# Rotary division on GpSimd in the narrow attentions of a two-layer decoder on one core

## The reference, cut

```python
# self: 32 query heads, 8 key heads, causal, rotary by halves of a head
q = rope(x @ Wq); k = repeat(rope(x @ Wk), 4); v = repeat(x @ Wv, 4)
w = softmax(where(causal, -inf, q @ k.T) / 4);  out = (w @ v) @ Wo
# cross: 32 key heads from ctx, no mask, rotary by pairs, angles from fside
q = rope2(x @ Wq); k = rope2(ctx @ Wk); v = ctx @ Wv
w = softmax(q @ k.T / 4);  out = (w @ v) @ Wout + bout
```

## Time and profile before

| | us |
|---|---|
| median of 3 runs | 3669.28 (3666.15 to 3674.68) |
| profiled execution, its own time | 3672.33 |
| its span | 3670.5 |
| TensorE busy | 3299.7 (90%) |
| VectorE busy | 2050.8 (56%) |
| ScalarE busy | 1330.1 (36%) |
| GpSimd busy | 569.7 (16%) |

### The profile page before, as it was taken

The page is one execution under the profiler, slowest core; times in us unless marked ns, Lnnn a source line. Parts: engine busy times, 40 slices in busy tenths (PEclk is TensorE's granted clock), DMA queues, the critical chain, the costliest instruction groups (busy, mean ns, idle before and its releaser), DMA issues. The chain is left out here.

```text
span 3670.5 us, 54520 instructions
## 1 busy us (share of the span) xinstructions
PE 3299.7 (90%) x19769; PEld 2526.3 (69%) x19770; DVE 2050.8 (56%) x4964; ACT 1330.1 (36%) x2944; POOL 569.7 (16%) x621
## 2 busy tenths in 40 slices
PE   6999999999999999977958899889898857999995
PEld 6888888888888788843425565555455435787784
DVE  3555655566666666651155666666666645443445
ACT  0444434443444344431113343435444442122110
POOL 1333322222222222033141111210000000000000
PEclk7999999999999999988978999989999978999998
DMA  5111111111011011034340000000000011000001
GB/s 190 53 53 53 53 53 30 35 35 30 30 35 35 27 33 30 1 117 163 130 140 2 2 3 2 28 2 22 5 5 5 2 46 24 24 11 11 23 11 46
DMA packets 110615, 146.79 MB, mean 40 GB/s; under 512 B 23712, under 2 KB 72864, under 8 KB 109288
## 3 DMA queue, kind: packets, MB, share of 16 engines
q1 hardware_dynamic: 95904, 110.80, 9.4%
q0 software_dynamic: 14480, 32.91, 2.9%
HBM read 100.55 MB, written 42.08 MB: 39 GB/s over the span
## 5 line engine op out<-in xcount | busy, mean ns | idle before, releaser
L554 ACT ACTIVATE probs_w<-probs_w,low_w 128x256 f32<-128x256 f32 (+1 forms) x512 | 242.9, 475 | 589.7 <-DVE low_w L599 589.7
L1871 DVE TENSOR_REDUCE mx_n<-bank 128x6 f32<-128x768 f32 (+1 forms) x256 | 279.7, 1093 | 151.0 <-PE bank L1648 83.0
L1779 ACT ACTIVATE probsT_n<-bank 128x768 f32<-128x768 f32 (+1 forms) x256 | 235.8, 921 | 277.0 <-PE bank L1660 276.8
L572 DVE TENSOR_TENSOR probsT_lo_w<-bank,probsT_hi_w 128x384 fp32r<-128x384 f32 (+1 forms) x256 | 159.7, 624 | 125.7 <-ACT probsT_hi_w L537 124.9
L518 PE MATMUL bank<-wo_hi_w,oT_hi_w 128*128 128x512 f32 x512 | 211.4, 413 | 2.1 <-issue 2.1
L1642 PE MATMUL bank<-kT_n,qT_n 48*128 48x256 f32 (+1 forms) x1024 | 124.0, 322 | 94.2 <-DVE mx_n L1871 91.5
L518 PE MATMUL bank<-wo_hi_w,oT_lo_w 128*128 128x512 f32 x512 | 204.4, 399 | 0.0
L518 PE MATMUL bank<-wo_lo_w,oT_hi_w 128*128 128x512 f32 x512 | 204.4, 399 | 0.0
L582 DVE TENSOR_SCALAR probs_w<-probs_w,inv_w 128x256 f32<-128x256 f32 (+1 forms) x512 | 187.6, 408 | 20.8 <-issue 0.9
L2309 DVE SCALAR_TENSOR_TENSOR h<-bank,scale_now,silu 128x512 f32<-128x512 f32 x64 | 48.0, 750 | 202.5 <-PE bank L2202 202.5
L450 PE MATMUL bank<-xT_lo_w,wq_hi_w 128*128 128x512 f32 x512 | 161.1, 396 | 0.0
(11 more groups left out here) (362 smaller groups left out, 8141.3 us busy)
## 6 DMA issues: line engine op xcount, KB each, us to landing
expert_rows<-ctxT_hi_w SPq DMA_DIRECT2D x20, 512.0 KB, 4.3
work_m<-expert_rows SPq DMA_DIRECT2D x40, 256.0 KB, 2.6
expert_products<-work_m POOLq DMA_DIRECT2D x40, 256.0 KB, 2.7
staging_w<-in_L_attn_Wq SPq DMA_DIRECT2D x32, 256.0 KB, 3.0
expert_table<-ctxT_hi_w SPq DMA_DIRECT2D x16, 512.0 KB, 5.5
staging_w<-in_L_attn_Wo SPq DMA_DIRECT2D x32, 256.0 KB, 2.6
staging_w<-in_L_xattn_Wq SPq DMA_DIRECT2D x32, 256.0 KB, 2.6
staging_w<-in_L_xattn_Wo SPq DMA_DIRECT2D x32, 256.0 KB, 2.6
```

Of the source, the lines that this page charges most:

```text
L554: last = act.activation(pr, pr, ACT.Exp, bias=low[:, n % ROUNDS_OF_PROBS, tile:tile + 1], scale=-1.0, accum_out=den[:, n % ROUNDS_OF_PROBS ...
L572: return dve.tensor_tensor(dst, src, hi.bitcast(FP32), ALU.subtract)
L1779: act.activation(probsT[:, turn_ % SLOT_PAIRS, :, 0:cols], scoreT[:, :, 0:cols], ACT.Exp, scale=SCALE)\
L1871: dve.tensor_reduce(to.rearrange("p t h -> p h t"), seen, AX.X, ALU.max).then_inc(s["scores_read"], 1)
```

## The change

The second half of a rotation moves from VectorE to GpSimd. VectorE keeps the three products that read the bank, and tells by a new semaphore `turned` that they are done. GpSimd's new `divide` makes the sum, the rounding and the remainder and sets `split`. `rot` and `turn` get two buffers, taken in turn by the number of the rotation (k0, k1, q0, q1 of each item), and VectorE waits before a rotation until the one two before it is divided. The wait for the transposes of the keys, before parts of q are written, moves along. GpSimd now goes through the steps as the other engines do: at each step first `hide` (self items), then the divisions of that step, then context loads at step 11, then the weight loads. `var`, `rstd` and `newton` become slices of one tile.

```diff
-    rot, turn = sb("rot", [P, DIM]), sb("turn", [P, DIM])
+    rot, turn = sb("rot", [P, 2, DIM]), sb("turn", [P, 2, DIM])
+    rotation = lambda name, n: 4 * n + (2 if name[0] == "q" else 0) + int(name[1])
...
+            def divide(name, n):
+                t, q = int(name[1]), name[0] == "q"
+                heads_ = NH if q else kv_heads(n)
+                r, u = (by_head(a, name, n) for a in (rot, turn))
+                pool.wait_ge(s["turned"], rotation(name, n) + 1)
+                pool.tensor_tensor(r, r, u, ALU.add)
+                if q:
+                    pool.wait_ge(s["prep_ready"], max(uses.ready[f"kT{t}{i}", n] for i in turns(n)))
+                pool.drain()
+                twice = r.unsqueeze(2).to_broadcast([P, heads_, 2, HW])
+                if q or cross(n):
+                    d = parts[:, t, :, :].rearrange("p h (a w) -> p h a w", w=HW)
+                    hi, lo = d[:, :, 0:3:2, :] if q else d[:, :, 0:2, :], d[:, :, 1 if q else 2, :]
+                    pool.tensor_copy(hi.bitcast(FP32R), twice)
+                    pool.drain()
+                    last = pool.tensor_tensor(lo, r, d[:, :, 0, :], ALU.subtract)
+                else:
+                    d = parts[:, t, 0:2 * heads_, :].rearrange("p (h c) (a w) -> p c h a w", c=2, w=HW)
+                    for i in range(2):
+                        pool.tensor_copy(d[:, i, :, 0:2, :].bitcast(FP32R), twice)
+                    pool.drain()
+                    for i in range(2):
+                        last = pool.tensor_tensor(d[:, i, :, 2, :], r, d[:, 0, :, 0, :], ALU.subtract)
+                last.then_inc(s["split"], 1)
...
+            for n in range(-1, ITEMS):
+                for at in range(PAIRS):
+                    if 0 <= n < BATCH:
+                        hide(n, at)
+                    early, late = step(n, at)
+                    for name, item in early + late:
+                        if name in ("k0", "k1", "q0", "q1"):
+                            divide(name, item)
+                        elif name == "ctxT" and batch_of(item) + 1 < BATCH:
+                            load_context(batch_of(item) + 1)
...
+                if turn_ >= 2:
+                    dve.wait_ge(s["split"], turn_ - 1)
                 dve.tensor_tensor(r, b, wide(cos, HW), ALU.mult)
...
                 last.then_inc(s["prep_dve"], 1)
-                dve.drain()
-                dve.tensor_tensor(r, r, u, ALU.add)
-                dve.drain()
...
+                dve.drain().then_inc(s["turned"], 1)
```

More of the change, by code:

```diff
@@ L1490, in attention_narrow @@
     ident16, own16 = sb("ident16", [P, P], BF16), sb("own16", [P, P], BF16)
-    stat, var, rstd, newton = sb("stat", [P, TILES, 8]), sb("var", [P, TILES]), sb("rstd", [P, TILES]), sb("newton", [P, TILES])
+    stat, roots = sb("stat", [P, TILES, 8]), sb("roots", [P, 3, TILES])
+    var, rstd, newton = (roots[:, i, :] for i in range(3))
     score, scoreT = chip.banks[0], chip.banks[1]
@@ L1498, in attention_narrow, with by_head @@
     half = lambda h, rows: slice(64 * (h % 2), 64 * (h % 2) + rows)
+    rotation = lambda name, n: 4 * n + (2 if name[0] == "q" else 0) + int(name[1])
+    def by_head(a, name, n):
+        heads_ = NH if name[0] == "q" else kv_heads(n)
+        return a[:, rotation(name, n) % 2, 0:heads_ * HW].rearrange("p (h w) -> p h w", w=HW)
     masked = lambda bank: bank.rearrange("p (a b) -> p a b", b=SEQ)[:, :, 0:P]
@@ L1506, in attention_narrow @@
             "wq_cross_loaded", "wk_cross_loaded", "wv_cross_loaded", "wo_cross_loaded", "bias_loaded", "ctx_loaded", "consts_ready",
-            "prep_ready", "prep_act", "prep_dve", "split", "scores_ready", "scores_read", "neg_ready",
+            "prep_ready", "prep_act", "prep_dve", "turned", "split", "scores_ready", "scores_read", "neg_ready",
             "negA_there", "negB_there", "negC_there", "scoresT_ready", "exp_ready", "hidden", "values_ready", "heads_copied", "x_ready")}
@@ new lines, in _ @@
+            pool.wait_ge(s["consts_ready"], 1)
+            for name, n in before:
+                if name in ("k0", "k1"):
+                    divide(name, n)
+            for n in range(-1, ITEMS):
[8 more added lines that the diff above has]
+                            load_context(batch_of(item) + 1)
+                    if (n, at) == (BATCH - 3, PAIRS - 1):
@@ L1554, in _ @@
                         pool.wait_ge(s["prep_ready"], uses.ready["k1", BATCH - 1])
                         pool.dma_start(wk(BATCH), k_dram.rearrange("(c p) n -> p c n", p=P)).then_inc(s["wk_cross_loaded"], 16)
-                    if (n, pair) == (BATCH - 2, 7):
+                    if (n, at) == (BATCH - 2, 7):
                         pool.wait_ge(s["prep_ready"], uses.ready["q1", BATCH - 1])
                         pool.dma_start(wq[:, :, :], q_dram.rearrange("(c p) n -> p c n", p=P)).then_inc(s["wq_cross_loaded"], 16)
-                    if (n, pair) == (BATCH - 2, PAIRS - 1):
+                    if (n, at) == (BATCH - 2, PAIRS - 1):
@@ L1560, in _ @@
                         pool.wait_ge(s["prep_ready"], uses.ready["v1", BATCH - 1])
                         pool.dma_start(wv(BATCH), v_dram.rearrange("(c p) n -> p c n", p=P)).then_inc(s["wv_cross_loaded"], 16)
[L1562 to L1566, removed]
+                    if (n, at) == (BATCH, 7):
+                        pool.wait_ge(s["prep_ready"], uses.ready["out1", BATCH - 1])
+                        pool.dma_start(wo[:, :, :], o_dram.rearrange("(c p) n -> p c n", p=P)).then_inc(s["wo_cross_loaded"], 16)
@@ L1830, in rotate @@
                 wide = lambda a, w: a.unsqueeze(1).to_broadcast([P, heads_, w])
-                r = rot[:, 0:width].rearrange("p (h w) -> p h w", w=HW)
-                u = turn[:, 0:width].rearrange("p (h w) -> p h w", w=HW)
+                turn_ = rotation(name, n)
+                r, u = (by_head(a, name, n) for a in (rot, turn))
+                if turn_ >= 2:
+                    dve.wait_ge(s["split"], turn_ - 1)
                 dve.tensor_tensor(r, b, wide(cos, HW), ALU.mult)
```

## The result

The changed kernel takes 3625.8 us in the median of four runs (3616.0 to 3627.2), against 3670.7 us for the kernel before: a ratio of 0.987, 95% interval [0.985, 0.988]. So it is faster by 1.2 to 1.5%, 45 us, where 54 us were forecast. The profiled execution took 3627.2 us, its span is 3625.4 us.

What follows compares the result with a forecast made beforehand. TensorE was taken to bound the narrow attentions, waiting for maxima late on VectorE. Terms 5 + 8 + 3 + 15 + 27 - 4 = 54 us took the profiled 3672.3 us to 3618, as median 3615; range 3572 to 3655.

Steps and rivals of the forecast that it cites:

- What bounds: Narrow attentions: TensorE bounds, so a change on VectorE is worth only what TensorE waits for it.
- GpSimd's division: Sum, rounding and remainder of a 512-wide rotation on GpSimd: 4.1 us with the handover, against 2.3 us on VectorE.
- rival 2: GpSimd's four-dimensional operations on 16-element rows cost more than flat ones: 3640 us (chance 0.12) or 3680 us (0.10).
- Start: Before the first scores nothing covers the latency of GpSimd's divisions in a row: 4 us lost.
- Cross k: Key rotations of cross items: scores wait less for maxima, one slow-clock stretch goes; 3.4 us x 8 = 27 us gained.
- Cross q0: q0 rotation of cross items: earlier negations, idle split in two, half the slow clock recovered; 15 us gained.
- Self q0: q0 rotation of self items: values start 0.6 us earlier, slow clock stays; 5 us over 8 items.
- Self k: Key rotations of self items: waits for maxima go, 0.4 us returns at the negation; 8 us gained.
- First item behind q1: First self item: the 3.26 us wait behind q1 goes, with no hide in the way; 3 us gained.
- The lock: SBUF held exclusively for a whole GpSimd instruction: each VectorE negation operation can lose a whole GpSimd operation.
- Signs named ahead: Expected profile marks: shorter maxima wait, new negation and values waits, slower negations, granted clock 0.97 cross, about 0.92 self.
- Rival 1: Negations slip between GpSimd's operations and the clock recovers everywhere: 106 us gained, 3563 us; chance 0.20.

Runs made afterwards that it cites:

- twice: The full change with GpSimd's 1024-element rounding made a second time in each division: 3656.5 us, 0.995.
- cross_k: The full change with only the keys of the cross items divided on GpSimd: 3639.1 us, 0.991.
- cross_only: The full change with only the rotations of the cross items divided on GpSimd, those of the self items on VectorE: 3617.3 us, 0.986.
- self_only: The full change with only the rotations of the self items divided on GpSimd: 3671.1 us, 0.999.
- q0_later: The full change, but GpSimd divides q0 one step later, behind hide 1 and after that step's negations: 3581.8 us, 0.975.
- k_yield: `q0_later`, with GpSimd also waiting between sum and rounding of k0 until the negations of pair 5 are done: 3595.9 us, 0.980.
- hide_first: `q0_later` without the wait for the negations, so GpSimd divides q0 right after hide 1: 3614.3 us, 0.984.

## Why the prediction was right, and where not

The mechanism held in the cross items, where all of the gain lies; the term of the self items failed, and that the sum came out near is in part luck.

- **What bounds.** Right: VectorE lost 110 us of busy time and ScalarE none, and only what TensorE waited and the clock behind its waits turned into time.
- **GpSimd's division**, 4.1 us taken: 3.8 us from the sum's start to the remainder's end (2151.17 to 2155.01). Right, and rival 2 with it fell: no operation on short rows was slow. `twice` puts its turning point at an estimated 5.6 us, near the 5.5 that I named; at 5.0 us a division it took more than the half of the gain that I gave it.
- **Start**, 4 us: 5.1 us. The missing 1 us is that the projections of q0 and q1 took 8.05 us where they had taken 7.03: from 1934.1 to 1942.2 us the granted clock is 0.87, in the same work before it was 1.00.
- **Cross k**, 27 us: 34 to 36 us (`cross_k`). The mechanism was right, the term too small, and by its idle time: over items 7 to 14 TensorE idles 21 us less, where 1.3 us in each of 8 items, 10 us, were counted; its busy time fell by 15 us, where 17 were counted for the clock. The lock held one negation operation per place, not two: L1908 ran 1.02 us once and L1910 0.18 us, so TensorE's transposes waited 0.26 us and not 1.3; kT10 waited 0.74 us, for ScalarE's copies as taken into account.
- **Cross q0**, 15 us: 18 to 21 us (`cross_only` less `cross_k`), which the intervals do not tell from 15. The waits after are 0.68 and 0.85 us where 1.0 and 1.1 stood. By stretch TensorE idles 10 us less (8 counted) and is busy 8 us less (7 counted).
- **Self q0**, 5 us: with self k nothing in items 1 to 6 (`self_only`). The step was right in its parts: negations and hide each come late, 2.6 us idle instead of 3.23, slow clock unchanged. But 0.2 us of the 0.6 went as TensorE was busy longer (52.9 us in an item instead of 52.7; why, no run shows), and the rest into the k part.
- **Self k**, 8 us: nothing in items 1 to 6. This step failed; only its 2 us for the first item can have come (below). I asked what is late next and answered with the negations alone; behind them stands their DMA into the queries. Before the change an item shows one such wait, of 0.5 us, at another place; now there is a second, of 1.1 us, behind k1, which is what k1's wait gave up. The negation transposes wait 0.5 us there, as the 0.4 that I counted. In item 2 the new DMA wait is 2.9 us, and this item has two slow stretches and takes 61.6 us; why that DMA took longer, no run shows. Waits of one self item, before and then after:

```profile
PE bank L1642 <- DVE mx_n L1871: 4.4, 3, 3.2
PE bank L1660 <- DMA qT_n<-negT_n: 0.5, 1, 0.5
PE bank L1642 <- ACT xT_n L1742: 0.3, 1, 0.3
```
```profile
PE bank L1704 <- DMA qT_n<-negT_n: 1.5, 2, 1.1
PE bank L1727 <- issue: 1.5, 1, 1.5
PE bank L1670 <- DVEq L1911: 1.3, 2, 0.8
PE bank L1686 <- DVE mx_n L1896: 0.3, 1, 0.3
```

- **First item behind q1**, 3 us: item 0 gained 5.6 us in all, so this and the 2 us for its k were right in sum. But a hide was in the way: behind q1 TensorE waits 0.40 us for the maxima and then 1.38 us for GpSimd. Items 1 to 6 together lost 2.5 us, 3.5 of it in item 2.
- **The sum**, 54 us, against 45: two errors that met, self items 13 us too high (16 for 3) and cross items 9 us too low (42 for 51), and 5 us more lost at the start and outside the narrow part. That the median landed within 11 us of the forecast is in part luck.
- **The lock.** The row it rested on and the section "Who interferes with whom" of the Trainium skill's page "SBUF — State Buffer" hold here too: L1910 at 0.85 us beside the rounding, 0.18 us when GpSimd waits. The trace agrees with a hold for the whole instruction. What I got wrong is how often: an operation is held only if GpSimd's next one begins before it. Of the 120 negation operations of the narrow part 32 took over 0.3 us after the change, 17 in `q0_later`, and 1 before.
- **Signs named ahead.** The wait for the maxima under 25 us (12.1), negation transposes some 20 us (18.4), values product some 20 us (15.8, two rows), clock 0.97 in the cross stretch (0.97) were right. L1908 and L1910 over 0.5 us in the mean was wrong: 0.34 and 0.42 us, and only the L1910 of 16 columns is over it (0.79). So the sign of being wrong, negations that keep 0.18 us, came in part: most of them kept it.
- **Rival 1** (negations slip through, clock recovers) was not how this kernel ran, but `q0_later` came near it by another order of the work: 3582 us, where the rival had 3563.

## What to carry to other kernels

When work moves to an idle engine, list for that engine what is queued behind it, for the old one which small operations it now holds up (0.18 us became 0.85 here), and for the engine that bounds what it waits for next. Put the moved work behind all of them where its own deadline allows: here one step of delay and one wait, for a result that is due four steps later, were worth as much (44 us) as the whole move (45 us). A delay without that room costs: `k_yield` lost 14 us by one. And value an idle of TensorE by the clock behind it too: removing one of two short waits gave 0.4 us at most in an item whose slow stretch stayed, removing both gave 3.9 us.

## What was not expected of the hardware

Idle time of TensorE in pieces was followed by the lower clock as one long idle was: behind 0.31, 0.80 and 1.51 us, with 0.8 and 0.4 us of work between them, stands the same half-clock stretch as behind 3.23 us in one piece, and behind 0.32 and 1.11 us (`q0_later`) none. In `hide_first` 0.31 and 1.2 us at this place were followed by a slow stretch in four self items and by none in two, so the same pattern of work can meet either clock. GpSimd rounds 1024 elements in 1.04 us and 512 in 0.61 us, so a second half costs 0.43 us; VectorE takes 0.69 us for the 1024, and for this operation the two engines are closer (1.5 times) than for the two-input ones (1.27 against 0.69 us, 1.8 times).
